# Where the scores stand in a step of the last cross attention

## The reference

```python
def _L3_xattn_ref(query, context, w_q, w_kv, w_out, b_out):
    q = query @ w_q
    kv = context @ w_kv
    k, v = jnp.split(kv, 2, axis=-1)
    ... # each in 16 heads of 64
    scores = jnp.einsum('bhqd,bhkd->bhqk', q, k) * SCALE
    attn = jax.nn.softmax(scores, axis=-1)
    out = jnp.einsum('bhqk,bhkd->bhqd', attn, v)
    return out @ w_out + b_out

x = x + jnp.tanh(g_xattn[3]) * _L3_xattn_ref(_layernorm(x, axis=-1), ctx_768, ...)
```

## Time and profile before

| | us |
|---|---|
| median of 3 runs | 2292.95 |
| lowest and highest of them | 2291.43, 2298.33 |
| the profiled execution | 2296.02 |
| its span in the profile | 2294.2 |
| stage of the last cross attention, about | 1735 to 2211 |

### The profile page before, as it was taken

How to read it: one execution, slowest core, us unless ns; L and a number is a source line. 1 busy time by engine, 2 the same in 40 slices (tenths; PEclk the granted TensorE clock), 3 DMA queues, 4 the chain that set the end, 5 groups by cost and what they waited for, 6 DMA issues and landing times. The chain is left out here.

```text
span 2294.2 us, 49158 instructions
## 1 busy us (share of the span) xinstructions
PE 2004.6 (87%) x18068; PEld 1514.7 (66%) x18068; DVE 1571.2 (68%) x3190; ACT 1250.2 (54%) x2832; POOL 796.4 (35%) x698
## 2 busy tenths in 40 slices
PE   6669999999996998969999977777997999999964
PEld 3359999899994666646666644665684666666653
DVE  5789999999997888734544445554575566666644
ACT  3279888888871676723333215754422566666631
POOL 1124445444461333225444444331000333333233
PEclk7589999999997999979999988997998999999975
DMA  2100000000002000044533520001000000000001
GB/s 59 43 1 8 14 9 14 9 14 15 8 8 77 9 9 6 2 92 94 123 81 75 117 42 15 4 1 52 1 1 11 1 4 5 9 4 1 1 2 37
DMA packets 41418, 61.81 MB, mean 27 GB/s; under 512 B 9464, under 2 KB 18208, under 8 KB 40800
## 3 DMA queue, kind: packets, MB, share of 16 engines
q1 hardware_dynamic: 41184, 58.66, 10.6%
HBM read 56.02 MB, written 2.62 MB: 26 GB/s over the span
## 5 line engine op out<-in xcount | busy, mean ns | idle before, releaser
L827 POOL TENSOR_TENSOR a_probs<-a_probs,a_rsums 128x1024 f32<-128x1024 f32 x64 | 121.3, 1896 | 321.3 <-DVE a_rsums L875 321.3
L1510 POOL TENSOR_TENSOR f_h<-f_gated,f_w_spread 128x512 f32<-128x512 f32 x128 | 161.6, 1268 | 196.7 <-DVE f_gated L1564 93.7
L1564 DVE TENSOR_TENSOR f_gated<-f_silu,f_up 128x512 f32<-128x512 f32 x128 | 87.1, 686 | 184.3 <-PE f_up L1641 169.4
L2336 ACT ACTIVATE f_combine<-f_logits,f_neg_row_max 128x128 f32<-128x128 f32 x512 | 198.5, 396 | 0.7 <-DVE f_neg_row_max L2194 0.7
L1604 ACT ACTIVATE f_silu<-f_gate 128x512 f32<-128x512 f32 x128 | 76.2, 597 | 221.2 <-PE f_gate L1641 218.0
L2155 POOL TENSOR_TENSOR f_slot_sum<-f_slot_sum,f_logits 128x512 f32<-128x512 f32 x96 | 122.7, 1278 | 182.2 <-DVE f_slot_max L2273 99.1
L2163 POOL TENSOR_TENSOR f_acc<-f_acc,f_row_factor 128x512 f32<-128x512 f32 x128 | 136.2, 1066 | 60.5 <-DVE f_slot_max L2273 38.4
L1656 PEld LDWEIGHTS f_acc<-f_down,f_h 128*128 128x128 f32 x1024 | 128.9, 192 | 42.6 <-issue 37.8
L2397 PE MATMUL f_give_bank<-f_y,f_combineT 128*128 128x128 f32 x1024 | 140.7, 281 | 12.8 <-DVE f_y L2243 7.4
L863 DVE TENSOR_REDUCE a_negmax<-a_score_bank 128x8 f32<-128x1024 f32 x64 | 78.2, 1222 | 102.9 <-PE a_score_bank L1004 102.9
L2386 PE MATMUL f_slot_bank<-f_logits,f_xn 128*128 128x128 f32 x1024 | 136.5, 276 | 6.0 <-issue 5.1
(11 more groups left out here) (327 smaller groups left out, 4997.3 us busy)
## 6 DMA issues: line engine op xcount, KB each, us to landing
f_w_spread<-f_routing_rows SPq DMA_DIRECT2D x64, 512.0 KB, 9.9
f_w<-in_f_w SPq DMA_DIRECT2D x16, 256.0 KB, 2.5
a_cT<-in_ctxT SPq DMA_DIRECT2D x16, 192.0 KB, 2.5
f_gate_up<-in_f_guT SPq DMA_DIRECT2D x1, 2048.0 KB, 8.1
out<-x_resident SPq DMA_DIRECT2D x8, 256.0 KB, 2.4
c_cT<-in_ctxT SPq DMA_DIRECT2D x8, 192.0 KB, 2.5
a_ctx<-in_ctx SPq DMA_DIRECT2D x8, 192.0 KB, 2.6
f_phi<-in_f_phi SPq DMA_DIRECT2D x1, 1024.0 KB, 5.9
```

The lines of the kernel that those rows point to most:

```text
L827: nc.gpsimd.tensor_tensor(probs[:, u], probs[:, u], rsums[:, u, :].unsqueeze(2).to_broadcast([S, 8, S]), ALU.mult).then_inc(normalised, 1)
L1510: nc.gpsimd.tensor_tensor(h[:, u % KEPT, :], gated[:, u % 2, :], w_spread[:, u // PER, u % PER, :], ALU.mult).then_inc(weighted, 1)
L2336: last = nc.scalar.activation(back[:, m % BACKS, j, :], raw[:, m % RING, j, :], ACT.Exp, bias=neg_row[:, k, b:b + 1], accum_out=row_part[: ...
```

## The change

Two edits in this stage, both in the order within a step; nothing is computed otherwise, and no instruction is added or taken away.

PE: in a step the order was turn(p+1), projection, scores(p+3), projection, mix (even steps), weigh(p), projection. It becomes turn(p+1), projection, projection, mix, weigh(p), scores(p+3), projection. The wait for emptied projections that the scores of the next group need in steps 5 and 6 goes with the scores.

ACT: in a step the order was copy(p+1), two emptied projections, exponentials(p+3), keep(p), one emptied projection. It becomes exponentials(p+2), copy(p+1), two emptied projections, keep(p), one emptied projection. Exponentials of pair 2 stood before the groups, and now stand first in step 0, which is the same place. DVE, POOL and SP are as before.

```diff
--- before.py
+++ after.py
@@ -950,19 +950,18 @@
                 exponentiate(FIRST, 0)
                 exponentiate(FIRST, 1)
                 copy_turned(FIRST, 0)
-                exponentiate(FIRST, 2)
 
                 def group(at, before, after, after2):
                     for p in range(PAIRED):
+                        pair = pair_at(at, after, p + 2)
+                        if pair:
+                            exponentiate(*pair)
                         pair = pair_at(at, after, p + 1)
                         if pair:
                             copy_turned(*pair)
                         if after:
                             for n in projections_of(p)[0:2]:
                                 empty(after, n)
-                        pair = pair_at(at, after, p + 3)
-                        if pair:
-                            exponentiate(*pair)
                         keep_out(at, p)
                         if after:
                             empty(after, projections_of(p)[2])
@@ -1059,12 +1058,6 @@
                             turn(*pair)
                         if after:
                             project_ahead(after, mine[0])
-                        if after and p in (5, 6):
-                            pe.wait_ge(emptied, it * PROJECTIONS + (8, 16)[p - 5] + 2)
-                        pair = pair_at(at, after, p + 3)
-                        if pair:
-                            scores(*pair)
-                        if after:
                             project_ahead(after, mine[1])
                         if p == 0 and before:
                             mix(before, G - 1)
@@ -1075,6 +1068,11 @@
                         if p == 0:
                             pe.wait_ge(emptied, it * PROJECTIONS + 2)
                         weigh(at, p)
+                        if after and p in (5, 6):
+                            pe.wait_ge(emptied, it * PROJECTIONS + (8, 16)[p - 5] + 2)
+                        pair = pair_at(at, after, p + 3)
+                        if pair:
+                            scores(*pair)
                         if after:
                             project_ahead(after, mine[2])
                         if after2 and p == TURN_NORM_AT:
```

## The result

The changed kernel takes 2310.15 us, median of 9 runs (2302.15 to 2318.88), against 2292.95 for before on the same chip: a ratio of 1.0077, 95% interval 1.0060 to 1.0094, so +17.2 us. Forecast were 2312.4 and +19.4, with 2302 to 2323 as the range.

The account below looks back on a forecast made before the run. PE was taken to bound the kernel, with the scores-to-turn chain hidden but close to showing. Long part 9.1, last group 7.1 and clock 3.2 gave +19.4 on the median 2292.95, so 2312.4 us, range 2302 to 2323.

Parts of the forecast that it names:

- Chain against room: Scores to turn takes 8.53 us, but PE has 7.92 between them from an even step: the turn waits 0.61.
- Two steps in the long part: Seven groups with projections: two steps take 14.13 us instead of 13.71, +9.1 us over 28 stretches.
- The step with the norm: Step 5, whose four transposes add 0.44 on PE: 14.13 against 14.15, so -0.02 us per stretch.
- Weighing to scores: New distance between starts on PE, taken at 1.03 us, bounds 0.86 and 1.10.
- The rule on drains: Changing tiling mode drains TensorE; three changes a step instead of four, saving 0.19 per two steps, without effect behind the chain.
- ACT's edit, taken at nothing: Exponentials moved first on ACT don't delay the chain; the emptying behind them is covered by 0.4 us; cost 0.
- The last group: Group without projections, every chain showing: turn 1 to turn 7 takes 36.93 us instead of 29.83, +7.1.
- The clock: In the last group PE idles longer; two falls of the granted clock on the path, +3.2 us.
- The rival that the clock falls in every group of the long part: One fall in each of seven groups, 11 us more, 2323.5 us; chance 0.08.
- The sum: Chain in seven groups, last group and clock: 9.1 + 7.1 + 3.2 = +19.4 us.
- 3.35 us to spare: Slack of the hidden chain in before: turn at 1948.68 less scores at 1936.80 and 8.53.
- the 3.96 taken away: Even-step scores move 3.77 later behind the turn and two steps get 0.19 shorter; less 3.35 leaves 0.61.

Follow-up runs that it names:

- after_half: The changed kernel, but with GpSimd (POOL) normalising only four of a pair's eight heads; 2292.41 us, one execution.
- last_early: The changed kernel, but in the last group, without projections, the scores stand directly behind the turn as before; 2305.16 us, ratio to before 1.0043.
- mix_first: Against before: PE does turn, two projections, mixing, scores, weighing, projection, ACT exponentials first; last group in before's order on both; 2285.63 us, ratio 0.9971.
- fill: The changed kernel plus 2, 3 and 4 unread projections behind the scores of steps 1, 3 and 5 of the last group; 2311.06 us, ratio to before 1.0068.
- act_only: Before with the edit on ACT alone, the scores left where they were; 2296.88 us, ratio 1.0026.
- pe_only: The changed kernel with ACT's order of before, so the edit on PE alone; 2469.93 us, one execution.
- two_then_scores: Against before: PE does turn, two projections, scores, mixing, weighing, projection, with ACT as in the changed kernel; 2293.99 us, ratio 1.0004.
- before_half: Before, but with GpSimd (POOL) normalising only four of a pair's eight heads; 2290.80 us, one execution.

## Why the prediction was right, point by point

- *Chain against room.* Right in mechanism: turns of even steps wait for POOL, those of odd steps don't. Foretold was that the turn comes 0.61 later than PE's own parts would let it; measured 6.39 - 5.77 = 0.62 in the loop and 6.48 - 5.77 = 0.71 in the written-out groups. (The profile's idle time, 0.46 and 0.55, is less by 0.16, since it counts from the modelled end of the projection before.) That it came so near is in part luck. Two numbers were off a little and in the same direction: PE's parts are 5.77 in an odd step, not 5.87 (after_half), and the chain is 8.44 in the loop, not 8.53, since the turn starts 0.05 behind POOL there and not 0.14. The section on the change names a weighing and a mixing as what left the way from the scores of step 2 to the turn of step 4; the second projection left it as well, and it takes all three (1.88 + 1.02 + 0.86) to make the 3.77 by which the scores moved.
- *Two steps in the long part.* Foretold 14.13; measured 14.00 in the loop's groups (6.39 + 7.61) and 14.06 in the others (6.48 + 7.58). The step with the norm was foretold at no loss and indeed is no longer than the others now: the norm's transposes fall into the wait. The stretch from that turn to the next scores was 5.60, measured 5.56. The sum of this term was 9.1, measured 7.26, and of that some 1.5 is not the chain: in after's profile the clock fell behind the loop's jump. Where it did not, in last_early, with the same order in these groups, the long part is 5.76 above before. So for the chain alone the term was some 3 us too high. PE was foretold to be 96% busy, and is 97% (53.59 of 55).
- *Weighing to scores.* Taken at 1.03, measured 1.02 (1905.72 to 1906.74) and 1.03 (1897.48 to 1898.51). What was too dear were the parts behind two projections: projection to weighing is 0.95 there and not 1.06, projection to mixing 0.86 and not 0.96. I had carried over what they cost behind scores.
- *The rule on drains.* The saving exists: without the wait the new order is 13.32 for two steps against 13.71 (after_half). It is 0.39, twice my 0.19, and mix_first collects it. In after itself the chain eats it, as foretold. The count of changes of shape fits the steps of all orders better than my distances did: a step is 0.19 or 0.20 shorter where it has three changes instead of four (last section). That a drain is the cause is not shown; no run changes a shape and leaves the order.
- *ACT's edit, taken at nothing.* In after it holds: the waits view of the long part has no wait of PE for ACT, and fill's last group comes to 37.02 where the chain alone gave 36.93. Alone it is not free in the last group (act_only), which the text didn't see. That it belongs to the first edit was right: without it the long part is 142 us longer (pe_only).
- *The last group.* 36.93 foretold without the clock, 37.02 measured without it (fill), and the chain of 8.53 or 8.54 stands three times in after itself. One inner reading was off: turn 2 was put at 6.48, with scores 2.05 before turn 1. Turn 1 waits for POOL as well, so the scores start 2.77 before it and turn 2 comes at 5.76. The path does not go through turn 2, but the idle time before turn 3 was put too low by it, at 2.7 where 3.39 was measured.
- *The clock.* The mis-sized term: 3.2 foretold, 5.9 measured (41.15 - 37.02 and 16.24 - 14.43). The two falls that were foretold cost 2.50 and 1.64, not 1.6 each, and there was a third, around turn 7, that cost 1.8 in the tail, where I had put nothing. The rival that the clock falls in every group of the long part did not come true; it fell once there, behind the loop's jump.
- *The sum.* 9.1 + 7.1 + 3.2 = 19.4 against 7.26 + 7.19 + 5.94 = 20.4 in the profiled stage. The long part was too high and the clock too low, and they nearly cancel: that the sum came within 1 us is luck, the mechanism is not. The interval of the ratio is +14 to +22 us, so the median's +17.2 contradicts neither sum.

## What to carry to other kernels

A hidden chain has a length and a room; before moving its head back, add up what the bounding engine does between its head and its tail, for each kind of step, since the one that leaves the least room decides. Here 3.35 us to spare were less than the 3.96 taken away. And when a producer moves, its consumer on another in-order engine must move with it, and each must be checked where the filler work ends: the last group without projections lost, with its tail, 13.1 us, the seven others together 7.3.

## What the runs showed of the hardware

- What a part costs on PE depends on the part before the last: from a projection to the weighing it is 1.06 when scores stand before the projection, 0.95 behind another projection (1896.53 to 1897.48); from the mixing to the weighing 1.88 behind a projection, 1.98 to 1.99 behind scores.
- A step is shorter by 0.19 or 0.20 where the shape changes three times between its parts instead of four. Odd steps: 5.96 with four changes (before, act_only), 5.77 with three (after_half, two_then_scores, mix_first). Even steps: 7.75 with four (before, act_only, two_then_scores), 7.55 with three (after_half, mix_first).
- The tail does the same work in all eleven kernels. It took 14.42 or 14.43 us in the four whose granted clock was 1.00 around turn 7 (before, fill, before_half, two_then_scores), and 16.05 to 17.16 in the seven where it fell to 0.50 there. The length of the last wait alone does not tell the two apart: PE waited 3.28 us before turn 7 in act_only, where the clock fell, and in two_then_scores, where it stayed.
- The wake-up of a turn by POOL is not one number. In the loop's groups it is 0.05 us; in the groups written out ahead of the loop and behind it, it is 0.15, as in these two rows of after:

```profile
2140.43 1.90 POOL L827 TENSOR_TENSOR a_probs<-a_probs,a_rsums 128x1024 f32<-128x1024 f32 x1 [6.40 <-DVE a_rsums L875]
2142.48 1.06 PE L1013 MATMUL a_turn_bank<-ident,a_probs 128*128 128x128 f32 x8 [0.55 <-POOL a_probs L827]
```

- Where the loop over the groups jumps back, PE stands still for about 2 us and waits for nothing that the profile shows, in before as well (in this profile the step is 8.05 instead of 5.96):

```profile
2006.06 1.09 PE L1014 MATMUL a_turn_bank<-ident,a_probs 128*128 128x128 f32 x8 [1.93 <-issue]
```

  In after the wait is 2.03, this step is 7.96 and the next 9.12 instead of 7.61, for there the clock fell behind the wait; the window of after from 2002 to 2004 shows it:

```profile
2002.00:2004.00 2.00, 2.00 (x6) 1.19 (x5) 0.81 (x2) 1.02 (x1) 1.00 (x1) 0.53 0.00 0
```

  It fell there in fill (8.52 and 10.48) and before_half (7.83 and 9.43) too, and not in before, last_early or mix_first. The Trainium skill (Runtime: NRT & Kernel Launch, Instruction fetch mechanics) says that a taken branch whose target is not in the fetched pages costs a fetch; the place agrees, and no run here took the loop away to show the cause.
